# Forward transforms four quads behind the outputs instead of three, and one load issued earlier, in a spectral attention block

## The chip, the cores and the metric

The kernel runs on one core of a Trainium2 chip. The metric is the device time of one execution in microseconds (us), median of several runs; lower is better.

## The reference

The input x is (4, 64, 256, 256) in float32: four batches of 64 images of 256 x 256 pixels. Cut to what matters:

```python
def _spec_conv(x, w1, w2, out_hw, bias=None):
    xf = jnp.fft.rfft2(x, norm='forward')
    ... # keep the lowest modes, multiply by w1 and w2
    y = jnp.fft.irfft2(out_ft, s=(Ho, Wo), norm='forward')

def tno_forward(x, ...):
    xa_n = _inorm(xa, norm1_w, norm1_b)
    k, q, v = ... # three _spec_conv of every image, 8 x 8 modes
    dprod = softmax(einsum('batd,basd->bats', q, k) * 64)   # 64 x 64 images of one batch
    att = einsum('bats,basd->batd', dprod, v)
    att = _inorm(att, an_w, an_b) + xa
    att_n = _inorm(att, norm2_w, norm2_b)
    mix = _spec_conv(att_n, mix_w1, mix_w2, (H, W), bias=mix_bias)   # 32 x 32 modes
    mixed = _inorm(mix + skip, mix_norm_w, mix_norm_b)
    return _inorm(mixed, mon_w, mon_b) + att

x = x + tno_forward(_gn(x), ...)      # _gn: group norm over width groups of 8, all images of a batch
```

The attention of a batch and its group norm need all 64 images of the batch, so nothing of a batch can be put out before the last image of it has been transformed.

## The kernel before

All 64 images of a batch lie in SBUF in one buffer X (128 partitions, two rows of the image each). A pair is two images (32 pairs, 512 KB each), a quad is four (16 quads). There is only one X: an image of the next batch is loaded over an image of this batch once that one has been stored.

TensorE (PE in the profile) does for each pair a `forward` (L342, sixteen records in the trace on L350, X times the Fourier table into a bank of psY). ScalarE (ACT) squares the images (L554) and copies psY into Y (`keep_y`, L546), and VectorE (DVE) sums the squares (L872). When all pairs of a batch are through, `attend` computes the norms, the 64 x 64 attention on low modes and the first coefficients. Then `produce` (L492 on PE, L1110 on DVE, L643 on ACT) walks over the quads with a counter u:

- for u in 0 to 15, PE does `inverse_w` twice (L404) and `inverse_h` of the next quad once (L389), GpSimd (POOL) scales the four images in X (L784), and VectorE adds the synthesis from PSUM to X (`finish`, L836; semaphore `out_made`). `inverse_w(s)` waits for `out_made` of image 2s - 3, because it reuses four PSUM banks.
- from u = LAG on, PE also does the `forward` of two pairs of the next batch ahead of these inverses; those forwards go on until u = 15 + LAG. LAG is 3. In the last batch there are no such forwards.

So a produce has three phases: a head (u below LAG) with inverses alone, a middle with both, and a tail (u above 15) with forwards alone. Which comes first on each engine is written out by hand. Some work of the second group of coefficients hangs on the same counter through `second(b)`, which is LAG in all but the last batch: `energy`, `spread` and `turn_low` on PE at second, second + 3 and second + 4, `deviations`, `coefficients`, `keep_spread` and `add_low` on DVE at second to second + 4, and `low_piece(b, 2)` on ACT at second + 5, whose result `inverse_h` of quad 10 reads at u = 9. POOL waits for `coef_made` before image 4 * LAG + 12 (L799).

All image transfers are issued by SyncE (SP) on one queue: `store` waits for `out_made`, `reload` waits for the store of the same pair. After store q of a batch comes the reload of pair q - 1. The first and the last two pairs are moved in halves of one image.

There are three places where a batch hands over to the next. They are called the first, second and third handover here; the last batch has none. In the first its head begins at about 115 us and its tail ends at 232 us of the span.

Of the kernel before, what the change touches and what calls it, by code (L numbers as in the profile page):

```python
# [13 lines left out]
U0 = 8  # L14
PAIRS, QUADS, NG = IMGS // 2, IMGS // 4, IMGS // 8
TABLES = 15
LAG = 3
RING = 4
QRING = 8
HALVED = (0, PAIRS - 2, PAIRS - 1)  # L20
# [54 lines left out]
def spectral_block(nc, x, mix_re, mix_im, mix_mirror, low_w, low_mix, scalars,  # L75
# [8 lines left out]
    with ctx:  # L84
# [158 lines left out]
        def second(b):  # L243
            return LAG if b < B - 1 else 1

# [29 lines left out]
        @block.sync  # L275
        def _(sp):
            def load_images(nb, n0, n1, done):
                sp.dma_start(Xf[:, n0:n1, :], x_v[nb, :, n0:n1, :]).then_inc(done, 16)

            def store_images(b, n0, n1, done):  # L280
                sp.wait_ge(out_made, 64 * b + n1)
                sp.dma_start(out_v[b, :, n0:n1, :], Xf[:, n0:n1, :]).then_inc(done, 16)

            def load(nb, q):
                if q in HALVED:
                    load_images(nb, 2 * q, 2 * q + 1, load_first[q])
                    load_images(nb, 2 * q + 1, 2 * q + 2, load_done[q])
                else:
                    load_images(nb, 2 * q, 2 * q + 2, load_done[q])

            def reload(nb, q):
                if q in HALVED:
                    sp.wait_ge(store_first[q], 16 * nb)
                    load_images(nb, 2 * q, 2 * q + 1, load_first[q])
                    sp.wait_ge(store_done[q], 16 * nb)
                    load_images(nb, 2 * q + 1, 2 * q + 2, load_done[q])
                else:
                    sp.wait_ge(store_done[q], 16 * nb)
                    load_images(nb, 2 * q, 2 * q + 2, load_done[q])

            def store(b, q):
                if q in HALVED:
                    store_images(b, 2 * q, 2 * q + 1, store_first[q])
                    store_images(b, 2 * q + 1, 2 * q + 2, store_done[q])
                else:
                    store_images(b, 2 * q, 2 * q + 2, store_done[q])

            flat = lambda t: t.rearrange("p r n -> p (r n)")
            small = [(GWT[:, :, :, :, :].rearrange("p a b n v -> p (a b n v)"), t_w), (flat(INVH[:, :, :]), t_inv_h),
                     (INVW[:, :], t_inv_w), (GROUP[:, :], t_group), (EYE[:, :], t_eye), (SEL[:, :], t_sel),  # L310
                     (SIDE[:, :], t_side), (PAIR[:, :], t_pair), (ROWS[:, :], t_rows), (SC[:, :], scalars),
                     (MRE, mix_re), (MIM, mix_im), (MMIR, mix_mirror), (flat(LM[:, :, :]), low_mix),
                     (LW[:, :, :, :].rearrange("p n r k -> p (n r k)"), low_w)]
            sp.dma_start(FWD[:, :, :].rearrange("p a n -> p (a n)"), t_fwd).then_inc(fwd_in, 16)
            for q in range(PAIRS):
                load(0, q)
                for dst, src in small[5 * q - 40:5 * q - 35] if q >= 8 else ():
                    sp.dma_start(dst, src).then_inc(tables_in, 16)  # L318

            def batch(b, more):  # L320
                for q in range(PAIRS - 2):
                    store(b, q)
                    if more and q:
                        reload(b + 1, q - 1)
                for q in range(PAIRS - 2, PAIRS):
                    store(b, q)
                for q in range(PAIRS - 3, PAIRS) if more else ():
                    reload(b + 1, q)

            for b in range(B):  # L330
                batch(b, b < B - 1)
            for q in range(PAIRS):
                sp.wait_ge(store_done[q], 16 * B)
            for q in HALVED:
                sp.wait_ge(store_first[q], 16 * B)
# [3 lines left out]
        def _(pe):  # L339
            mm = nc.tensor.matmul  # L340

            def forward(nb, p):  # L342

                if not (isinstance(nb, int) and nb == 0 and p < 2):
                    pe.wait_ge(y_kept, 32 * nb + p - 1)
                for i in range(2):
                    pe.wait_ge(loaded(2 * p + i), 16 * nb + 16)
                    for c in range(WC):
                        for a in range(HC):
                            last = mm(psY[p % 2][:, (2 * i + c) * 128:(2 * i + c + 1) * 128],  # L350
                                      X[:, 2 * p + i, a, c * 128:(c + 1) * 128], FWD[:, a, :],
                                      start=a == 0, stop=a == HC - 1)
                last.then_inc(y_made, 1)

            def add_squares(nb, k):

                if nb:
                    pe.wait_ge(t_kept, 32 * (nb - 1) + min(2 * (k + LAG + 1) + 2, 32))
                pe.wait_ge(q_summed, 64 * nb + 4 * k + 4)
# [132 lines left out]
            def produce(b, more):  # L492
                for u in range(QUADS + (LAG if more else 0)):
                    new = more and u >= LAG
                    if new:
                        if u == LAG:
                            pe.wait_ge(mode_weighted, 8 * b + 8)
                        forward(b + 1, 2 * (u - LAG))
                        if u == LAG + 1:
                            pe.wait_ge(var_made, 2 * b + 2)  # L500
                        if u == LAG + 4:
                            pe.wait_ge(c2_kept, 2 * b + 2)
                        if u == LAG + 5:
                            pe.wait_ge(d_added, 6 * b + 6)
                        forward(b + 1, 2 * (u - LAG) + 1)
                    if new and u > LAG:
                        add_squares(b + 1, u - LAG - 1)
                    if u < QUADS:
                        inverse_w(b, 2 * u)
                        if u + 1 < QUADS:  # L510
                            inverse_h(b, u + 1)
                        if new and u in (LAG, LAG + 3, LAG + 4):
                            pe.wait_ge(y_kept, 32 * (b + 1) + 2 * (u - LAG) + 2)
                        if u == second(b):
                            energy(b, 1)
                        if u == second(b) + 3:
                            spread(b, 1)
                        if u == second(b) + 4:
                            turn_low(b, 1)
                        inverse_w(b, 2 * u + 1)  # L520
                if more:
                    add_squares(b + 1, QUADS - 1)
# [665 lines left out]
```

## Time and profile before

| | |
|---|---|
| median of 3 runs | 677.81 us (675.39 to 679.09) |
| profiled execution | 681.9 us, span 679.9 us |
| mean granted TensorE clock | 0.984 of full speed |
| PE, PEld busy | 94%, 86% of the span |
| DVE, POOL, ACT busy | 72%, 52%, 49% |
| DMA queue of the images | 135.36 MB, mean 199 GB/s over the span |

The span is the stretch that the trace covers; the time of the same execution is 2.0 us longer. A busy share is a mean over stages with different limits: the DMA engines are idle in each attend and almost always busy in each produce.

### The profile page before, as it was taken

The page shows a single profiled execution, that of the slowest core. Times are in us where ns is not written, and L with a number is a line of the kernel's source. Part 1 is how long each engine was busy: PE and PEld are TensorE (multiplying, and loading weights), DVE is VectorE, ACT ScalarE, POOL GpSimd, SP SyncE. Part 2 cuts the span into 40 slices and gives each one's busy share as a digit, 9 for nine tenths or more (in the row PEclk, how much of TensorE's full clock was granted, in tenths as well). Part 3 has the DMA queues.
Part 4 walks back from the last instruction along what each step waited for, and adds up shares of the span by engine and source line. Part 5 has one row for each costly group of instructions (what it writes and reads, how often), then busy time and mean ns, then how long its engine had stood idle before and what let it go on. Part 6 is the DMA issues. An engine that isn't in the chain of part 4 may idle for free.

```text
span 679.9 us, 15103 instructions
## 1 busy us (share of the span) xinstructions
PE 636.5 (94%) x5736; PEld 581.6 (86%) x5736; DVE 487.8 (72%) x1099; ACT 334.3 (49%) x722; POOL 356.1 (52%) x430
## 2 busy tenths in 40 slices
PE   9999999899999799979999899989999989995984
PEld 9999998699999799869999789969899988994863
DVE  4667676688777567668777666857887666778896
ACT  6888142465666413255666523246566650433331
POOL 0350035959960013796993002398799000359995
PEclk9999999899999899999999999999999989999997
DMA  9990000998999200299999900059989960004786
GB/s 320 350 379 9 1 2 20 308 314 294 310 318 328 94 1 1 77 308 343 286 328 309 322 14 1 2 198 331 321 285 325 308 218 1 1 1 162 280 302 247
DMA packets 72071, 136.32 MB, mean 200 GB/s; under 512 B 5760, under 2 KB 6272, under 8 KB 72000
## 3 DMA queue, kind: packets, MB, share of 16 engines
q1 hardware_dynamic: 72000, 135.36, 58.5%
q8 instruction: 46, 0.75, 0.4%
q14 instruction: 25, 0.20, 0.1%
HBM read 68.23 MB, written 67.11 MB: 199 GB/s over the span
## 4 chain that ended last, share of the span: by engine, by line
PE 58%; DVE 15%; POOL 9%; DMA 8%; issue 3%; ACT 3%; SPq 3%; POOLq 0%; DVEq 0%; ACTq 0%
PE psY L350 23%; PE psP L404 12%; POOL X L784 7%; PE psY L373 6%; DMA X<-in_x 6%; PE psT L389 5%; PE psP L454 5%; DVE QP L872 4%; ACT SQ L554 2%; PE psP L373 2%; DVE Y L836 2%; DVE SQ L836 2%; DMA out<-X 2%; SPq L318 2%; DVE X L836 1%
## 5 line engine op out<-in xcount | busy, mean ns | idle before, releaser
L350 PE MATMUL psY<-FWD,X 128*128 128x128 f32 x2048 | 251.1, 281 | 17.5 <-DMA X<-in_x 17.4
L350 PEld LDWEIGHTS psY<-FWD,X 128*128 128x128 f32 x2048 | 238.8, 195 | 33.0 <-issue 33.0
L784 POOL TENSOR_TENSOR X<-X,ALPHA 128x512 f32<-128x512 f32 x244 | 254.7, 1080 | 21.7 <-DVE IM L1072 19.7
L872 DVE TENSOR_REDUCE QP<-SQ 128x32 f32<-128x512 f32 x256 | 162.1, 679 | 57.8 <-ACT SQ L554 57.8
L836 DVE TENSOR_TENSOR X<-X,psP 128x512 f32<-128x512 f32 x192 | 126.5, 684 | 59.9 <-PE psP L404 26.1
L554 ACT ACTIVATE SQ<-X 128x512 f32<-128x512 f32 x256 | 146.4, 622 | 21.1 <-DMA X<-in_x 14.4
L404 PE MATMUL psP<-INVW,T 64*128 64x256 f32 x768 | 141.3, 402 | 12.0 <-DVE X L836 11.3
L762 POOL TENSOR_TENSOR Y<-Y,OMEGA 128x256 f32<-128x256 f32 x32 | 25.3, 790 | 215.9 <-ACT Y L558 215.6
L404 PEld LDWEIGHTS psP<-INVW,T 64*128 64x128 f32 x768 | 92.9, 190 | 31.2 <-issue 16.0
L576 ACT ACTIVATE T<-psT,BIA,SCL 128x256 f32<-128x256 f32 x128 | 65.3, 560 | 110.3 <-PE psT L389 105.8
L546 ACT ACTIVATE Y<-psY 128x512 f32<-128x512 f32 x128 | 76.2, 596 | 60.4 <-PE psY L350 59.6
L373 PE MATMUL psY<-GWR,Y 128*128 128x128 f32 x768 | 93.2, 279 | 0.0
L373 PEld LDWEIGHTS psY<-GWR,Y 128*128 128x128 f32 x768 | 87.8, 192 | 4.1 <-issue 3.0
L404 PE MATMUL psB<-INVW,T 64*128 64x256 f32 x256 | 69.7, 393 | 0.0
L389 PE MATMUL psT<-INVH,Y 64*128 64x256 f32 x512 | 67.1, 378 | 0.0
L389 PEld LDWEIGHTS psT<-INVH,Y 64*128 64x128 f32 x512 | 51.3, 189 | 4.8
L767 POOL TENSOR_TENSOR Y<-Y 128x256 f32<-128x256 f32 x32 | 23.8, 743 | 47.1 <-DVE Y L836 47.1
L404 PEld LDWEIGHTS psB<-INVW,T 64*128 64x128 f32 x256 | 46.1, 188 | 0.0
L836 DVE TENSOR_TENSOR X<-X,psB 128x512 f32<-128x512 f32 x64 | 43.6, 682 | 3.1 <-POOL X L784 2.6
L454 PEld LDWEIGHTS psP<-GWR,Y 128*64 128x64 f32 x272 | 30.5, 204 | 2.4 <-DVE GWR L839 2.4
L563 ACT ACTIVATE Y<-Y 128x128 f32<-128x128 f32 (+2 forms) x44 | 12.9, 294 | 39.4 <-DVE Y L836 28.5
L454 PE MATMUL psP<-GWR,Y 128*64 128x64 f32 x272 | 31.1, 275 | 0.8 <-DVE GWR L839 0.8
(189 smaller groups left out, 478.8 us busy)
## 6 DMA issues: line engine op xcount, KB each, us to landing
X<-in_x SPq DMA_DIRECT2D x116, 512.0 KB, 5.5
out<-X SPq DMA_DIRECT2D x116, 512.0 KB, 4.4
X<-in_x SPq DMA_DIRECT2D x24, 256.0 KB, 5.2
out<-X SPq DMA_DIRECT2D x24, 256.0 KB, 3.7
INVH<-t_inv_h SPq DMA_DIRECT2D x1, 256.0 KB, 9.6
LW<-in_low_w SPq DMA_DIRECT2D x1, 204.0 KB, 6.6
GWT<-t_w SPq DMA_DIRECT2D x1, 192.0 KB, 9.9
FWD<-t_fwd SPq DMA_DIRECT2D x1, 128.0 KB, 2.1
```

The costliest lines, as they stand in the source:

```text
L350: last = mm(psY[p % 2][:, (2 * i + c) * 128:(2 * i + c + 1) * 128], X[:, 2 * p + i, a, c * 128:(c + 1) * 128], FWD[:, a, :], start=a == 0, ...
L373: last = mm(over(psM[g % 3][:, col:col + 1], [[256, 2], [1, 64]]), both[:, c, k, :], over(GWR[:, c, k, 0, 0:1], [[NV, 2], [1, 2 * NV]]), s ...
L389: last = mm(psT[h][:, 0:H], S[rows, q, part, :, :].rearrange("p j n -> p (j n)"), INVH[rows, part, :], start=part == 0, stop=part == 1)
L404: last = mm(out_bank(b, 2 * s + i)[:, W * a:W * (a + 1)], T[rows, s % 4, 128 * a:128 * (a + 1)], INVW[rows, :], start=True, stop=True)
L454: last = mm(ps[0:IMGS, col:col + 64], Y[:, c, k, :, U0 + n], GWR[:, c, 0, k:k + 2, :], start=c == 0, stop=c == WC - 1)
L546: nc.scalar.activation(Y[:, :, :, i0:i0 + 3:2, :].rearrange("p c k i u -> p i (c k) u"), psY[p % 2][:, :].rearrange("p (i n u) -> p i n u" ...
L554: nc.scalar.activation(SQ[:, n % RING, :], Xf[:, n, :], ACT.Square).then_inc(squared, 1)
L576: nc.scalar.activation(T[:, p % 4, :], psT[p % 2][:, 0:H], ACT.Identity, bias=BIA[:, p:p + 1], scale=SCL[:, p:p + 1]).then_inc(t_kept, 1)
L762: P.tensor_tensor(v, v, over(OMEGA[:, 0:1], [[0, 4], [0, 2], [1, NV]]), MUL).then_inc(powers_weighted, 1)
L784: P.tensor_tensor(v, v, al, MUL).then_inc(x_scaled, 1)
L836: return V.tensor_tensor(out, a, b, op)
L872: V.tensor_reduce(QP[:, 4 * (k % 2) + place(n) % 4, :], SQ[:, n % RING, :].rearrange("p (a g j) -> p g a j", a=HC, j=GW), AX.XY, ADD).then ...
```

## The change

LAG becomes 4. The head of the first three batches is then four quads long, the middle has twelve quads instead of thirteen, and the tail has four quads of forwards instead of three. The steps that hang on second(b) and on LAG move one quad later with it: so does POOL's wait for `coef_made`, from image 24 to image 28. In the store and reload loop, reload 29 is issued between the stores of pair 30 and those of pair 31, instead of after both.

```diff
-LAG = 3
+LAG = 4
...
             def batch(b, more):
-                for q in range(PAIRS - 2):
+                for q in range(PAIRS):
                     store(b, q)
                     if more and q:
                         reload(b + 1, q - 1)
-                for q in range(PAIRS - 2, PAIRS):
-                    store(b, q)
-                for q in range(PAIRS - 3, PAIRS) if more else ():
-                    reload(b + 1, q)
+                if more:
+                    reload(b + 1, PAIRS - 1)
```

On PE, at the end of the first head, the program before runs the inverses of quad 2 and then the first forwards of batch 1 (rows on L350; L404 is `inverse_w`, L389 `inverse_h`).

```order
L404 MATMUL psP<-INVW,T 128x256 [waits out_made,t_kept]
L404 MATMUL psB<-INVW,T 128x256
L404 MATMUL psP<-INVW,T 128x256
L404 MATMUL psB<-INVW,T 128x256
L350 MATMUL psY<-FWD,X 128x128 [waits load_first0,y_kept,mode_weighted]
L350 MATMUL psY<-FWD,X 128x128 x3
L350 MATMUL psY<-FWD,X 128x128 [waits load_done0]
L350 MATMUL psY<-FWD,X 128x128 x3
L350 MATMUL psY<-FWD,X 128x128 [waits load_done1,y_kept]
```

In the changed kernel (its lines are two lower: L402, L387, L348) the same place reads as follows.

```order
L402 MATMUL psP<-INVW,T 128x256 [waits out_made,t_kept]
L402 MATMUL psP<-INVW,T 128x256 x3
L387 MATMUL psT<-INVH,Y 128x256 [waits t_kept]
L387 MATMUL psT<-INVH,Y 128x256 x3
L402 MATMUL psP<-INVW,T 128x256 [waits out_made,t_kept]
L402 MATMUL psB<-INVW,T 128x256
L402 MATMUL psP<-INVW,T 128x256
L402 MATMUL psB<-INVW,T 128x256
L348 MATMUL psY<-FWD,X 128x128 [waits load_first0,y_kept,mode_weighted]
L348 MATMUL psY<-FWD,X 128x128 x3
L348 MATMUL psY<-FWD,X 128x128 [waits load_done0]
```

The eight matrix products of quad 3's two `inverse_w` and the four of `inverse_h` now stand ahead of the first forward, which itself is unchanged and waits for the same loads.

On SP, at the end of a batch, the program before has the following.

```order
L278 DMA X<-in_x 128x2x512 [waits store_done28]
L282 DMA out<-X 128x512 [waits out_made] x4
L278 DMA X<-in_x 128x2x512 [waits store_done29]
L278 DMA X<-in_x 128x512 [waits store_first30]
L278 DMA X<-in_x 128x512 [waits store_done30]
```

The changed kernel has this in its place.

```order
L278 DMA X<-in_x 128x2x512 [waits store_done28]
L282 DMA out<-X 128x512 [waits out_made] x2
L278 DMA X<-in_x 128x2x512 [waits store_done29]
L282 DMA out<-X 128x512 [waits out_made] x2
L278 DMA X<-in_x 128x512 [waits store_first30]
```

The load of pair 29 no longer stands behind the two stores of pair 31, and those two now stand behind it.

## Rows read from the trace of the kernel before

**Rows 1.** The page's first part: busy us, share, instructions.

```profile
PE 636.5 (94%) x5736; PEld 581.6 (86%) x5736; DVE 487.8 (72%) x1099; ACT 334.3 (49%) x722; POOL 356.1 (52%) x430
```

**Rows 2.** Waits of all engines: us in total, times, longest us.

```profile
PE psY L350 <- DMA X<-in_x: 17.4, 9, 3.2
```

**Rows 3.** Waits of SP's own queue, same columns.

```profile
SPq L282 <- DVE X L836: 416.6, 117, 73.3
```

**Rows 4.** PE's timeline, first handover's head: start, us, line, idle before.

```profile
124.59 2.02 PE L350 MATMUL psY<-FWD,X 128*128 128x128 f32 x16 [0.32 <-DMA X<-in_x]
128.63 2.73 PE L350 MATMUL psY<-FWD,X 128*128 128x128 f32 x16 [2.01 <-DMA X<-in_x]
...
135.39 3.84 PE L350 MATMUL psY<-FWD,X 128*128 128x128 f32 x32
...
142.07 3.84 PE L350 MATMUL psY<-FWD,X 128*128 128x128 f32 x32
```

**Rows 5.** PE's timeline, heads of the second and third handover.

```profile
295.36 2.02 PE L350 MATMUL psY<-FWD,X 128*128 128x128 f32 x16 [2.26 <-DMA X<-in_x]
...
300.51 3.73 PE L350 MATMUL psY<-FWD,X 128*128 128x128 f32 x31
...
307.19 3.06 PE L350 MATMUL psY<-FWD,X 128*128 128x128 f32 x25
...
458.87 2.02 PE L350 MATMUL psY<-FWD,X 128*128 128x128 f32 x16 [2.70 <-DMA X<-in_x]
...
470.70 2.50 PE L350 MATMUL psY<-FWD,X 128*128 128x128 f32 x20
```

**Rows 6.** DVE's timeline: finish of image 11 in the three heads.

```profile
129.20 0.69 DVE L836 TENSOR_TENSOR X<-X,psB 128x512 f32<-128x512 f32 x1 [0.35 <-POOL X L784]
...
294.78 0.69 DVE L836 TENSOR_TENSOR X<-X,psB 128x512 f32<-128x512 f32 x1 [0.34 <-POOL X L784]
...
458.96 0.69 DVE L836 TENSOR_TENSOR X<-X,psB 128x512 f32<-128x512 f32 x1 [0.34 <-POOL X L784]
```

**Rows 7.** PE's timeline, first and second tail: first quad, longest wait, end.

```profile
216.49 3.84 PE L350 MATMUL psY<-FWD,X 128*128 128x128 f32 x32
...
224.88 3.35 PE L350 MATMUL psY<-FWD,X 128*128 128x128 f32 x16 [2.54 <-DMA X<-in_x]
...
232.16 0.28 PE L361 MATMUL psT<-ONES,QP 128*128 128x1 f32 x2
...
381.61 3.84 PE L350 MATMUL psY<-FWD,X 128*128 128x128 f32 x32
...
390.69 2.02 PE L350 MATMUL psY<-FWD,X 128*128 128x128 f32 x16 [3.23 <-DMA X<-in_x]
...
396.35 0.28 PE L361 MATMUL psT<-ONES,QP 128*128 128x1 f32 x2
```

**Rows 8.** SP's timeline, end of the first handover's transfers.

```profile
216.52 2.32 SPq L282 DMA_DIRECT2D out<-X  x4
218.88 3.52 SPq L278 DMA_DIRECT2D X<-in_x  x5
```

**Rows 9.** Windows: busy us of each engine, granted clock, DMA share, GB/s.

```profile
121.00:138.00 17.00, 14.53 (x105) 12.30 (x106) 10.88 (x20) 8.04 (x19) 16.68 (x20) 0.90 1.00 328
143.00:216.00 73.00, 73.00 (x691) 66.90 (x691) 55.46 (x100) 46.48 (x89) 47.66 (x50) 1.00 0.92 308
```

**Rows 10.** Windows after the first and the second head's wait.

```profile
128.60:132.00 3.40, 3.37 (x20) 3.09 (x22) 3.05 (x6) 1.66 (x3) 3.40 (x4) 0.67 1.02 327
...
295.40:298.80 3.40, 3.40 (x30) 3.15 (x32) 2.69 (x6) 1.60 (x3) 3.40 (x4) 1.00 0.92 308
```

**Rows 11.** POOL's timeline at its wait for `coef_made`, first handover.

```profile
151.32 8.51 POOL L784 TENSOR_TENSOR X<-X,ALPHA 128x512 f32<-128x512 f32 x8 [7.10 <-DVE IM L1072]
```

**Rows 12.** Timelines of PE and ACT at u = 8, first handover.

```profile
163.94 3.84 PE L350 MATMUL psY<-FWD,X 128*128 128x128 f32 x32
...
165.47 0.28 ACT L563 ACTIVATE Y<-Y 128x96 f32<-128x96 f32 x1 [2.66 <-DVE Y L836]
```

## The prediction

> **What bounds the kernel now.** I read the page first. PE is busy for 94% of the span, far ahead of DVE with 72% [rows 1], so whatever does not remove idle time or slow clock from PE can hardly shorten the run. Next I asked the list of waits what stops PE. Its largest entry with a releaser that this change touches is the forward waiting for a load of X: 17.4 us in nine waits [rows 2]. The order in time shows that these sit at two places of every handover: two in the head, when the first pairs of the next batch have not yet landed, and one in the tail, when pair 29 has not. In between PE has no gap at all: in the 73 us from 143 to 216 it is busy for 73.00 us [rows 9]. SP on its side waits mostly for outputs (416.6 us, most of it in the attends, [rows 3]), so in the middle the transfers follow PE and not the other way round.
>
> The head is slower than PE alone would be. The finishes of its images are released by POOL's scaling [rows 6], which takes about 1.06 us an image (8.51 us for eight, [rows 11]). PE has some 3 us of work in such a quad (worked out below), so it idles there anyway.
>
> **What the change does to the head.** PE gets quad 3's inverses ahead of the first forward. Their last wait is for the finish of image 11, which the change does not touch: it ends at 129.20 + 0.69 = 129.9, 295.5 and 459.65 us [rows 6]. The second `inverse_w` then takes 1.1 us, so the first forward starts at 131.0, 296.6 and 460.75. By then both pairs have landed: PE began on pair 1 at 128.63, 295.36 and 458.87 right after its landing [rows 4, 5]. The two pairs take 3.8 us as in the undisturbed quads [rows 4]. The inverses that follow take 300.51 - (295.36 + 2.02) = 3.1 us at full clock [rows 5]. So u = 4 ends at 137.9, 303.5 and 467.65. Before, it ended at 142.07, 307.19 and 470.70 [rows 4, 5]. That is 4.2, 3.7 and 3.05 us earlier, 10.9 us in all. It is the size of one pair of forwards moved out (3.8 us) plus waits and slow clock saved, minus the extra time at POOL's pace.
>
> **What it does to the middle.** Eleven quads are left after u = 4 in both versions, with the same work, and I take their 74.4 us (142.07 to 216.49) as they are. Three covers are needed for that.
>
> The loads: pair 2 is wanted at 137.9 instead of 135.39. For every later pair it is the same: outputs, and with them stores and reloads, come 3.0 to 4.2 us sooner, and the forward comes one quad (6.7 us) later behind them, so each load has 6.7 us more between its pair's outputs and its use, and is used 2.5 to 3.6 us later on the clock than now.
>
> The third piece of low modes: `low_piece(b, 2)` moves from u = 8 to u = 9, and `inverse_h` of quad 10 reads it in that same u = 9. Before, ACT started it 165.47 - 163.94 = 1.5 us after PE's quad began [rows 12], and it is two such instructions of 0.28 us. PE wants it after two forwards and one `inverse_w`, 4.9 us after the quad began. Since it is ready 2.0 us after the quad began, the cover shrinks from a quad and more to 2.9 us, but does not vanish. Behind that wait would stand the rest of PE's quad and all stores.
>
> POOL's pause: it stood idle for 7.10 us before image 24 [rows 11]. It now does four more images (4.2 us at the rate of [rows 11]) first and pauses before image 28, one quad later, so the distance to the finish that reads the first image after the pause is unchanged.
>
> **What it does to the tail.** PE goes through four quads of forwards at 3.82 us, 15.3 us, if no load is late. Before it took 232.16 - 216.49 = 15.7 us in the first handover and 396.35 - 381.61 = 14.7 us in the second [rows 7]; the third is like the first (15.5). So the tail itself gives +0.5 at worst and -0.4 at best, together nothing. Are the loads in time? Pair 29 was issued at 218.88, 2.4 us after the tail began, and PE started on it 8.4 us after the tail began [rows 7, 8]. Now PE wants it 9.5 us after the tail began. The reordering brings its issue forward by about 1.2 us, the time between the second and the fourth store of that burst [rows 8]. The halves of pairs 30 and 31 are still gated by their own stores; they kept up with PE from 224.88 on, and are wanted 11.5 and 13.4 us into the tail. All have 1 to 3 us to spare, so the 2.5 and 3.2 us waits go. The reordering alone I therefore cost at nothing here: the longer tail covers it. The two stores of pair 31 that it passes are delayed by one issue of 0.4 us, inside that room. Without the longer tail it would be worth up to 1.2 us a handover.
>
> **The clock.** In the first head, PE's granted clock fell to half (1.2 GHz of 2.4) for about 3.4 us after the wait: the window of 128.6 to 132.0 shows a mean of 0.67 [rows 10]. From 128.63 to the next quad's forward it took 6.76 us, against 5.15 us in the second handover with a clock of 1.00 [rows 4, 5, 10]. Such a fall costs 1.6 us. In the first tail it did so too (forward of one pair 3.35 us against 2.02, [rows 7]), in the second it did not, after a longer wait. The changed head has one idle stretch instead of two, from the end of quad 2 to the finish of image 9. In the first handover that is from 124.59 - 0.32 = 124.3 [rows 4] to 129.9 less two finishes at POOL's pace, 127.8 [rows 6], or 3.5 us. Of the two waits in heads shown at [rows 4, 5] with 2.01 and 2.26 us the shorter was followed by a fall, and of the two in tails again the shorter; so it is a matter of chance here, half and half. I book one fall for the three new heads, +1.6 us, between nothing and three (4.8 us). The saved one of the first head is inside the 4.2 us above.
>
> The Trainium skill (TensorE: Matmul & The Clock Gate, Part 1) says that the array's clock is gated down when PE has not been busy lately, and that a loop that waits for DMA can swing between the two rates; by it three falls rather than one, 3.2 us less gain. This trace bears it out only in part: the second handover had waits of 2.26 and 3.23 us and kept a clock of 1.00.
>
> **The sum.** 10.9 us from the heads, 0 from the tails, 1.6 us back for the clock: 9.3 us. Against the profiled execution's 681.9 us that gives 672.6; the median of the runs lies 4.1 us lower, so I predict 677.8 - 9.3 = 668.5 us.
>
> **Rivals.**
>
> *Transfers bind.* In the head the DMA engines are full (share 1.00) at 328 GB/s, and the middle takes 308 with a share of 0.92 [rows 9]. Outputs now come 4.2 us sooner, 1.3 MB at 308 GB/s, and the queue can catch up by 20 GB/s times 73 us, 1.5 MB. That is just enough. If the rate can't rise over 308 at all, the last loads land when they do now: pair 29 at 224.8 in the first handover, where PE wants it at 212.3 + 9.5 = 221.8. The gain there falls by 3 us, similarly in the others: 3 us in all, 674.8. For it speaks the share of 0.92; against it that SP waits for outputs, that is, requests are missing and not bandwidth. In between lie 3 to 9 us.
>
> The Trainium skill (DMA: Bandwidth & Descriptors, Specifications) gives about 358 GB/s as the limit of HBM for one core. By that the room would be 50 GB/s, 3.6 MB, and this rival would be out. The measured 328 with engines full is less.
>
> *The clock falls in every new head and more often elsewhere.* Three falls: 10.9 - 4.8 = 6.1 us, 671.7. With none: 666.9.
>
> *Slower.* The one mechanism that could do it is the third piece at u = 9. If `low_piece` is ready later than PE's `inverse_h` wants it by d in each handover, the gain shrinks by 3d. It decides at d = 9.3/3 = 3.1 us, and for a loss over 0.5% (3.4 us) at d = 12.7/3 = 4.2 us, that is when it is ready 7.1 us later in its quad than now; with d = 5 the time would be 683.5 us. ACT does its two copies (L576) before it and they wait for PE's previous quad, so I see no reason for that [rows 12].
>
> *No effect.* If the extra head quad took a full 6.7 + 1 us because PE's inverses wait for more than POOL, each head's gain is 1 us or so, 3 us in all. The finish rows of POOL's pace speak against it [rows 6].
>
> **How the numbers follow.** My forecast (7 to 12 us gained): 0.62. Transfers bind, partly or wholly (1 to 6 us): 0.17. Falls in every head (about 6 us): 0.10. No effect or little (within 3.4 us): 0.06. Slower: 0.05. The range of 662.5 to 675 us takes in no fall and some gain from neighbouring runs below, and the whole of the transfer rival above. A measurement tells 0.5% (3.4 us) from no change. Faster by more than that: 0.62 + 0.10 + about half of the transfer rival and a bit, 0.83; within: 0.12; slower: 0.05.
>
> **What would show it.** In the new profile the forward's wait for X (17.4 us) should be near zero, PE should idle before `inverse_w` in the heads on DVE and POOL instead, each tail should last 15.3 us with no gap, and the distance between the first heads' end and the tails' begin should be unchanged. Loads late in the tail would show the transfer rival, a granted clock of 0.5 after the heads the second, a wait of `inverse_h` for ACT L563 the third. The prediction is wrong if the first forward does not start about 6 us later than now, or if the middle's quads get longer than 6.7 us.

## The result: 0.5% faster, not 1.4%

The median of 20 runs of the changed kernel is 676.5 us, of 20 runs of the kernel before 679.6 us. The ratio is 0.9951, 95% interval 0.9928 to 0.9974: 3.3 us (1.8 to 4.9), where 9.3 were forecast. The median also lies above the stated range of 662.5 to 675 us. The profiled execution took 675.3 us with a span of 673.4, 6.5 us less than the one before. That pair shows more than the medians do: the profiled execution before lies 2.3 us above the median of its 20 runs, the one after 1.2 us below its own.

The page after, first part, answers to [rows 1].

```profile
PE 637.8 (95%) x5736; PEld 582.5 (86%) x5736; DVE 490.0 (73%) x1099; ACT 333.2 (49%) x722; POOL 356.1 (53%) x430
```

PE is busy 1.3 us longer with the same 5736 records, in a shorter span, so some of its work has got slower. The last batch alone has 2.0 us of that, and cost no time: the windows from the end of the third tail to the end of the span, before and after, are as long as each other, at a lower granted clock (the column before the last two).

```profile
560.58:679.90 119.32, 98.93 (x893) 84.94 (x891) 91.43 (x221) 33.90 (x95) 75.79 (x84) 0.95 0.38 142
554.14:673.40 119.26, 100.89 (x893) 86.35 (x891) 91.41 (x221) 33.89 (x95) 75.69 (x84) 0.93 0.38 142
```

The list of waits after, between 110 and 600 us (the three handovers), has no row of PE waiting for X, where before there were 16.9 us in that stretch and 17.4 in the whole span [rows 2]. So what the change was made for came true. In its place PE waits for DVE; before and after, in the same stretch:

```profile
PE psP L404 <- DVE X L836: 0.4, 2, 0.2
PE psP L402 <- DVE X L834: 11.4, 5, 3.7
```

PE's timeline of the first head after answers to [rows 4]. The number in brackets is the idle time before the group.

```profile
127.72 1.19 PE L402 MATMUL psP<-INVW,T 64*128 64x256 f32 x8 [3.67 <-DVE X L834]
128.66 1.96 PE L387 MATMUL psT<-INVH,Y 64*128 64x256 f32 x8
...
132.20 3.84 PE L348 MATMUL psY<-FWD,X 128*128 128x128 f32 x32
...
139.17 3.84 PE L348 MATMUL psY<-FWD,X 128*128 128x128 f32 x32
```

One idle stretch of 3.67 us, then an `inverse_h` that takes 1.96 us instead of 1.03. The forwards start at 132.2, where the prediction had 131.0, and u = 4 ends at 139.17 (137.9). The other two heads have the same form, and the second is worse:

```profile
290.05 2.08 PE L402 MATMUL psP<-INVW,T 64*128 64x256 f32 x8 [3.67 <-DVE X L834]
291.88 1.95 PE L387 MATMUL psT<-INVH,Y 64*128 64x256 f32 x8
295.47 4.04 PE L348 MATMUL psY<-FWD,X 128*128 128x128 f32 x32
...
302.64 3.84 PE L348 MATMUL psY<-FWD,X 128*128 128x128 f32 x32
...
453.51 2.08 PE L402 MATMUL psP<-INVW,T 64*128 64x256 f32 x8 [3.67 <-DVE X L834]
...
464.65 3.84 PE L348 MATMUL psY<-FWD,X 128*128 128x128 f32 x32
```

The windows after each head's stretch answer to [rows 10]; the column after the busy times is the mean granted clock, 1.00 for 2.4 GHz and 0.50 for 1.2.

```profile
127.70:131.10 3.40, 3.38 (x20) 3.30 (x22) 2.14 (x4) 0.44 (x1) 3.40 (x5) 0.64 1.10 371
...
290.00:293.40 3.40, 3.35 (x16) 2.97 (x18) 2.13 (x4) 0.00 (x0) 3.40 (x5) 0.50 1.01 372
293.40:296.80 3.40, 3.40 (x21) 2.57 (x19) 1.82 (x3) 2.46 (x6) 3.24 (x5) 0.63 0.97 296
...
453.50:456.90 3.40, 3.39 (x18) 3.02 (x20) 2.17 (x4) 0.00 (x0) 3.40 (x5) 0.58 1.04 366
```

The clock fell to half in all three new heads, in the second for twice as long. The tail has no gap, which answers to [rows 7] (216.49 to 232.16 before):

```profile
213.59 3.84 PE L348 MATMUL psY<-FWD,X 128*128 128x128 f32 x32
...
228.65 0.28 PE L359 MATMUL psT<-ONES,QP 128*128 128x1 f32 x2
```

That is 15.06 us, and the other two tails took the same. The middle is as it was: 139.17 to 213.59 is 74.42 us, as from 142.07 to 216.49 before.

### The profile page after: what moved, and what is told of

It reads as the page before. It is cut to its first block, busy times and chain, and to the rows that moved or that the text cites. A ratio compares the mean times of both kernels' runs of the same rounds, so it can differ in the third digit from the quotient of the medians.

```text
span 673.4 us, 15100 instructions
## 1 busy us (share of the span) xinstructions
PE 637.8 (95%) x5736; PEld 582.5 (86%) x5736; DVE 490.0 (73%) x1099; ACT 333.2 (49%) x722; POOL 356.1 (53%) x430
## 4 chain that ended last, share of the span: by engine, by line
PE 53%; DVE 20%; POOL 17%; ACT 5%; issue 4%; DMA 1%; SPq 0%; POOLq 0%; DVEq 0%; ACTq 0%
PE psY L348 20%; POOL X L782 12%; PE psP L402 11%; DVE QP L870 9%; PE psT L387 5%; PE psP L452 5%; PE psY L371 5%; ACT SQ L552 4%; DVE Y L834 3%; PE psP L371 2%; DVE SQ L834 2%; DVE X L834 1%; POOL ALPHA L775 1%; POOL Y L765 1%; POOL ALPHA L772 1%
## 5 line engine op out<-in xcount | busy, mean ns | idle before, releaser
L348 PEld LDWEIGHTS psY<-FWD,X 128*128 128x128 f32 x2048 | 234.6, 192 | 14.8 <-issue 14.6
L348 PE MATMUL psY<-FWD,X 128*128 128x128 f32 x2048 | 245.8, 279 | 0.7 <-DMA X<-in_x 0.6
L402 PE MATMUL psP<-INVW,T 64*128 64x256 f32 x768 | 144.9, 410 | 20.5 <-DVE X L834 19.7
L760 POOL TENSOR_TENSOR Y<-Y,OMEGA 128x256 f32<-128x256 f32 x32 | 23.8, 744 | 207.3 <-ACT Y L556 207.0
L402 PEld LDWEIGHTS psP<-INVW,T 64*128 64x128 f32 x768 | 95.5, 194 | 41.0 <-issue 24.8
L402 PE MATMUL psB<-INVW,T 64*128 64x256 f32 x256 | 71.5, 401 | 0.0
L387 PE MATMUL psT<-INVH,Y 64*128 64x256 f32 x512 | 70.5, 393 | 0.0
L387 PEld LDWEIGHTS psT<-INVH,Y 64*128 64x128 f32 x512 | 53.7, 197 | 5.3
L765 POOL TENSOR_TENSOR Y<-Y 128x256 f32<-128x256 f32 x32 | 25.2, 786 | 47.6 <-DVE Y L834 47.6
L402 PEld LDWEIGHTS psB<-INVW,T 64*128 64x128 f32 x256 | 47.4, 194 | 0.0
```

The source lines that it names most:

```text
L387: last = mm(psT[h][:, 0:H], S[rows, q, part, :, :].rearrange("p j n -> p (j n)"), INVH[rows, part, :], start=part == 0, stop=part == 1)
L402: last = mm(out_bank(b, 2 * s + i)[:, W * a:W * (a + 1)], T[rows, s % 4, 128 * a:128 * (a + 1)], INVW[rows, :], start=True, stop=True)
L765: P.tensor_tensor(S[:, 2 * g:2 * g + 2, 0, :, :].rearrange("p q j n -> p q (j n)"), w[:, 0, :].rearrange("p (q n) -> p q n", q=2), w[:, 1, ...
```

## The experiments

Each kernel is compared with the kernel before on the same chip; the ratio and its 95% interval are given. The median of the kernel before in the three groups (e1 to e4, e5 to e8, e9 to e12) was 680.1, 680.3 and 681.0 us.

### The two edits apart

**e1**: the lag alone, against the kernel before.

```diff
-LAG = 3
+LAG = 4
```

> Only LAG is 4; the stores and reloads stand in the old order. Theory (the longer tail covers the loads, the order edit is hidden): no forward waits for X in the tails, each tail lasts 15.1 us as in the changed kernel, and the time is that of the changed kernel, ratio to before 0.995 within 0.002. Rival (the order edit carries the measured gain): a wait for X of 1 us or more in the tails and a ratio of 1.00.

Measured: 675.9 us, ratio 0.9957 (0.9936 to 0.9978), the same as with both edits. PE has no wait for X in the handovers, and its first tail has no gap:

```profile
214.03 3.84 PE L350 MATMUL psY<-FWD,X 128*128 128x128 f32 x32
...
229.09 0.28 PE L361 MATMUL psT<-ONES,QP 128*128 128x1 f32 x2
```

15.06 us again, without the order edit. The theory held in this trace: behind the longer tail the order edit is hidden. The clock fell in all three heads here too.

**e2**: the order of stores and reloads alone. The cut shows the edit against the changed kernel.

```diff
-LAG = 4
+LAG = 3
```

> Only the order edit, with LAG 3. Theory: pair 29 is issued some 1.2 us sooner, its wait in each tail falls from 2.5 to 3.2 us to 1.3 to 2 us, heads unchanged; 3 us less at most, ratio 0.996. Rival (the queue is full at the end of a batch and the load lands when it did): the waits in the tails are as before, ratio 1.00.

Measured: 674.3 us, ratio 0.9924 (0.9891 to 0.9956). That is 5.2 us less (3.0 to 7.4), by the ratio more than both edits give together, though the intervals overlap. The theory had 3 us at most, which the interval just takes in. PE's first tail in its timeline:

```profile
215.36 3.84 PE L348 MATMUL psY<-FWD,X 128*128 128x128 f32 x32
...
219.17 4.09 PE L348 MATMUL psY<-FWD,X 128*128 128x128 f32 x32
...
223.24 2.03 PE L348 MATMUL psY<-FWD,X 128*128 128x128 f32 x16
225.61 2.02 PE L348 MATMUL psY<-FWD,X 128*128 128x128 f32 x16 [0.33 <-DMA X<-in_x]
227.47 0.77 PE L359 MATMUL psT<-ONES,QP 128*128 128x1 f32 x4
```

The wait of 2.54 us ahead of pair 29 [rows 7] is gone; what is left is scattered over this tail in pieces of 0.3 us, and no fall of the clock follows. PE starts on pair 29 some 5.9, 6.8 and 7.0 us into the three tails, against 8.4, 9.1 and 8.5 before. That is more than the 1.2 us a handover that the prediction gave it. SP's timeline shows one half of it.

```profile
215.38 0.95 SPq L282 DMA_DIRECT2D out<-X  x2
216.98 0.39 SPq L278 DMA_DIRECT2D X<-in_x  x1
217.42 0.97 SPq L282 DMA_DIRECT2D out<-X  x2
```

The load of pair 29 is issued 1.6 us after the tail began, against 2.4 in [rows 8], and in the other two handovers 1.0 and 1.4 against 2.9 and 2.3. That is 1.2 us sooner on average, as the prediction had it, and 3.5 in all. The other half is the time from issue to landing, the last number of these rows: first the kernel before in its three handovers, then e2.

```profile
X<-in_x SPq DMA_DIRECT2D x1, 512.0 KB, 5.9
X<-in_x SPq DMA_DIRECT2D x1, 512.0 KB, 6.1
X<-in_x SPq DMA_DIRECT2D x1, 512.0 KB, 6.0
X<-in_x SPq DMA_DIRECT2D x1, 512.0 KB, 4.1
X<-in_x SPq DMA_DIRECT2D x1, 512.0 KB, 5.6
X<-in_x SPq DMA_DIRECT2D x1, 512.0 KB, 5.5
```

Together 2.8 us less, most of it in the first handover. The program now puts two half stores directly ahead of this load instead of four, which would explain it: over the four traces with the old order (before, e1, e4, e12) the same load took 5.9 us on average, over the ten with the new one 5.1. No run separates this from the earlier moment of issue. The prediction counted the earlier issue alone.

### The clock

**e3**: the changed kernel with idle matrix products between quad 2 and quad 3 of the first three batches. They write to psY[0], which nobody reads before the next forward overwrites it.

```diff
+            def fill(b, n, bank, free):
+                pe.wait_ge(mode_weighted, 8 * b + free)
+                for _ in range(n):
+                    mm(bank[:, 0:256], ONES[:, :], FWD[:, :, :].rearrange("p a n -> p (a n)"), start=True, stop=True)
...
+                    if more and u == 3:
+                        fill(b, 6, psY[0], 7)
                     if u < QUADS:
                         inverse_w(b, 2 * u)
```

> The changed kernel with six idle matrix products (3.0 us, the results are never read) on PE between quad 2 and quad 3 of each of the first three heads, where PE idles 3.67 us. Theory (falls of the clock in the three new heads, 1.3, 2.7 and 1.2 us, ate half of the forecast gain): the clock stays at 1.00 in those heads, first forwards start at 131.0 instead of 132.2 in the first handover, and the time is 5 us under the changed kernel's, ratio to before 0.987 to 0.989. Rival (the gain is lost elsewhere, and the falls fill time that POOL's pace would take anyway): clock stays up and the ratio stays at 0.995.

Measured: 672.1 us, ratio 0.9894 (0.9853 to 0.9934). The first head and the window behind its idle stretch:

```profile
124.13 2.86 PE L437 MATMUL psY<-FWD,ONES 128*128 128x256 f32 x12
127.88 1.13 PE L402 MATMUL psP<-INVW,T 64*128 64x256 f32 x8 [0.89 <-DVE X L841]
128.81 1.06 PE L387 MATMUL psT<-INVH,Y 64*128 64x256 f32 x8
131.00 3.84 PE L348 MATMUL psY<-FWD,X 128*128 128x128 f32 x32
...
137.97 3.84 PE L348 MATMUL psY<-FWD,X 128*128 128x128 f32 x32
```

```profile
127.70:131.10 3.40, 3.16 (x25) 2.48 (x25) 2.09 (x4) 1.19 (x4) 3.40 (x5) 1.00 1.10 384
```

With PE kept busy the clock stays at 1.00 in all three heads. The forwards start at 131.0 and u = 4 ends at 137.97, as the prediction worked out for full clock (131.0 and 137.9). The other two heads have the same form:

```profile
288.86 1.14 PE L402 MATMUL psP<-INVW,T 64*128 64x256 f32 x8 [0.90 <-DVE X L841]
298.95 3.84 PE L348 MATMUL psY<-FWD,X 128*128 128x128 f32 x32
450.05 1.14 PE L402 MATMUL psP<-INVW,T 64*128 64x256 f32 x8 [0.89 <-DVE X L841]
460.14 3.84 PE L348 MATMUL psY<-FWD,X 128*128 128x128 f32 x32
```

From the end of the stretch to the end of u = 4 all three heads take 10.09 us here. In the changed kernel they take 11.45, 12.59 and 11.14, which is 1.4, 2.5 and 1.0 us more, 4.9 in all. So the times worked out for the heads were right, and the falls are what the sum lacked. By the ratios e3 is 3.9 us below the changed kernel, with intervals that overlap a little. Waits for X of 2.0 us in all are back in its third tail.

**e4**: the kernel before with the same function at its two waits for X.

```diff
                     pe.wait_ge(y_kept, 32 * nb + p - 1)
+                if nb and p in (1, 29):
+                    fill(nb - 1, 4 if p == 1 else 5, psY[1], 8)
```

> The kernel before with idle matrix products in the two places of each handover where PE waits for X: four (2.0 us) before the forward of pair 1 and five (2.5 us) before that of pair 29, results never read. Theory: it removes the falls of the clock in heads and tails, of which the profile had three at 1.3 to 1.6 us, and adds at most 0.5 us where a wait was shorter than the filling: 3 to 4 us less, ratio 0.994 to 0.996. Rival (the kernel before keeps its clock in most runs): ratio 1.00 or above.

Measured: 675.4 us, ratio 0.9936 (0.9916 to 0.9957). That is 4.3 us less (2.9 to 5.7), about what the theory gave, and the trace shows no fall of the clock in the handovers, where the kernel before had three: in the first head and in the first and third tail.

**e8**: the changed kernel once more.

> The changed kernel itself on the same chip as the other three. By its 20 runs: ratio 0.995, mean clock 0.978 to 0.982, falls of the clock in all three new heads. If falls were chance, as the prediction took them, some head would keep its clock in this second trace.

Measured: 676.4 us, ratio 0.9950 (0.9931 to 0.9968). Its three heads in windows:

```profile
128.30:131.70 3.40, 3.36 (x21) 3.25 (x23) 2.13 (x4) 0.56 (x2) 3.40 (x5) 0.66 1.00 369
290.60:297.40 6.80, 6.77 (x33) 5.61 (x34) 3.97 (x7) 2.45 (x6) 6.64 (x9) 0.55 1.03 331
454.20:457.60 3.40, 3.40 (x18) 3.05 (x20) 2.17 (x4) 0.00 (x0) 3.40 (x5) 0.57 1.02 351
```

The same three falls, the second again the longer one. With e1 that makes nine heads of nine. The three traces repeat each other so closely that they are hardly nine separate draws, but half and half does not describe them. How many heads fall in the runs without a trace is not known: their mean granted clock goes from 0.974 to 0.986 in the changed kernel's 20 runs.

### POOL's part of the new idle stretch

**e5**: the changed kernel with POOL's last two small steps moved from ahead of image 8 to ahead of image 12.

```diff
-                behind = {2: SPLIT + 1, 8 if b < B - 1 else 3: SPLIT + 2}
+                behind = {2: SPLIT + 1, 12 if b < B - 1 else 3: SPLIT + 2}
...
-                    if u == (2 if more else 1):
+                    if u == (3 if more else 1):
                         fold_powers(b, SPLIT + 2)
```

> The changed kernel with POOL's last pair of small steps (weigh and add_products, 1.4 us) moved from ahead of image 8 to ahead of image 12, and DVE's fold of it from u = 2 to u = 3. Theory (in the new heads PE's idle stretch is set by POOL's scaling and these steps): the stretch falls from 3.67 to about 2.3 us, the first forward comes 1.4 us sooner in each head, and the clock falls less often or not at all; 4 to 7 us under the changed kernel, ratio to before 0.985 to 0.989. Rival (it is only moved to the next quad, where the same 1.4 us are paid by PE): ratio 0.995.

Measured: 670.8 us, ratio 0.9882 (0.9847 to 0.9917). The first head:

```profile
126.48 1.62 PE L402 MATMUL psP<-INVW,T 64*128 64x256 f32 x8 [2.31 <-DVE X L834]
127.83 1.98 PE L387 MATMUL psT<-INVH,Y 64*128 64x256 f32 x8
130.96 3.84 PE L348 MATMUL psY<-FWD,X 128*128 128x128 f32 x32
```

The stretch is 2.31 us as forecast and the forwards start 1.24 us earlier than in the changed kernel. But the clock fell in all three heads nevertheless, so the gain over the changed kernel, 4.6 us by the ratios, is about the three times 1.4 us of the shorter stretches; the theory was wrong on the clock. This kernel has no wait for X in the handovers. In the second head the fall lasted 3.4 us here, not 6.8.

**e6**: e5 with four idle products.

```diff
+                    if more and u == 3:
+                        fill(b, 4, psY[0], 7)
```

> As e5, with four idle matrix products (2.0 us, results never read) in the stretch that is left. Theory: no fall of the clock in the three heads, first forwards at about 129.6 us in the first handover; ratio 0.984 to 0.987. If e5 alone already keeps its clock, both are the same.

Measured: 668.7 us, ratio 0.9839 (0.9809 to 0.9869), with the clock at full in the three heads. It is the lowest ratio of the set, though its interval overlaps those of e5 and e7. **e10** repeats it:

> The best so far again: 0.984 to 0.986. With the heads 1.4 us shorter each, waits for X of about 1 us are left in some tails, since the transfers now follow closely.

Measured: 671.0 us, ratio 0.9849 (0.9798 to 0.9899). In its second tail waits for X are back:

```profile
384.75 2.02 PE L348 MATMUL psY<-FWD,X 128*128 128x128 f32 x16 [0.94 <-DMA X<-in_x]
...
389.11 2.02 PE L348 MATMUL psY<-FWD,X 128*128 128x128 f32 x16 [0.33 <-DMA X<-in_x]
```

In all it waits 4.7 us for X in the three handovers, and e6 waits 3.5. This suggests that the faster heads have used up the room in the transfers, but e5, whose heads are nearly as fast, has no such wait.

### Is the longer lag worth anything when the clock holds?

**e7**: the order edit with LAG 3, three idle products ahead of pair 1.

```diff
+                if nb and p == 1:
+                    fill(nb - 1, 3, psY[1], 8)
```

> The order edit with LAG 3 and three idle matrix products (1.5 us, results never read) ahead of the forward of pair 1 in each head, where PE waits 1.8 us for X. Theory (without falls of the clock the longer lag is still worth 2 to 3 us more than the order edit): ratio 0.990 to 0.992, above the 0.9894 of the filled kernel with LAG 4. Rival (the order edit is all that is needed): 0.989 or less.

Measured: 670.7 us, ratio 0.9867 (0.9839 to 0.9895). The rival on record was right: with the clock held, the order edit at LAG 3 is no worse than LAG 4 (e3, 0.9894). The intervals overlap, so three more kernels were run side by side.

**e9** is e3 again, **e11** is e7 again, and **e12** is e3 with the old order of stores and reloads.

> The filled kernel with LAG 4 and the new order again, beside the one with LAG 3. If the longer lag is worth something once the clock holds, this one is lower than the filled order edit by 2 us or more; the earlier runs had 0.9894 and 0.9867 the other way round, with overlapping intervals.

> The filled order edit with LAG 3 again: 0.987 if the longer lag is worth nothing with the clock held, 0.990 or more if it is.

> LAG 4 and the filling, with the stores and reloads in the old order. Theory (with the longer tail the order edit is hidden also when the heads are faster): as the same kernel with the new order, ratio 0.989, no wait for X of 1 us or more in the tails. Rival (faster heads bring the last loads close to PE): waits in the tails and 1 to 3 us more.

| | lag | order | fill | median us | ratio (95%) |
|---|---|---|---|---|---|
| e9 | 4 | new | yes | 671.6 | 0.9861 (0.9815 to 0.9907) |
| e11 | 3 | new | yes | 672.0 | 0.9861 (0.9816 to 0.9905) |
| e12 | 4 | old | yes | 672.0 | 0.9870 (0.9809 to 0.9931) |
| e4, from the first group | 3 | old | yes, at both waits | 675.4 | 0.9936 (0.9916 to 0.9957) |

Between the first three these runs can tell no difference. e12 had no wait of PE for X in the handovers, so its theory held as well. e9 waited 3.3 us for X, e11 7.4. The last row is the corner that is missing otherwise: the clock is held and neither edit is made. Its ratio, to the kernel before on its own chip, lies above those of e7, e9 and e11 beyond the intervals, and above those of e3 and e12 with intervals that overlap a little. So with the clock held the edits are still worth some 3 to 5 us.

In none of the fifteen new heads with idle products (e3, e6, e9, e10, e12) did the clock fall.

## Why the prediction was wrong

**What bounds.** Right. The waits for X in the handovers were 16.9 us before and none after.

**The heads.** The term was 10.9 us at full clock, 4.2 + 3.7 + 3.05. e3 confirms it: its first head ends within 0.1 us of the time worked out, and the other two take as long. What was wrong is the next term.

**The clock: the step that failed.** "I book one fall for the three new heads, +1.6 us." u = 4 ended at 139.17 in the first head (137.9 worked out), 1.3 us late. In the second it ended at 302.64; the worked-out 303.5, less the 3.5 us by which the first handover had ended sooner, is 300.0, so 2.6 us late. In the third it ended at 464.65 against 467.65 - 4.2 = 463.4, or 1.2 us late. Together 5.1 us instead of 1.6; the comparison with e3 gives 4.9.

The stretch the change would make was worked out in the prediction as 3.5 us in one piece (3.67 measured). It was then judged by waits of 2.0 to 3.2 us in the kernel before, which stood between forwards, and called chance. Among those waits the record is indeed mixed: after 2.01, 2.54 and 2.60 us the clock fell, after 2.26, 2.70 and 3.23 us it did not. The new stretch stands between inverses, and there it fell nine times of nine, and in e5 three times of three with 2.31 us, while with idle products in the stretch it never did. So the idle stretch is what brings the fall. That inverses around it make the difference to the waits of similar length is a guess that no run tested. The Trainium skill (TensorE: Matmul & The Clock Gate, Part 1) says that the array's clock is gated down when PE has not been busy lately. The changed kernel agrees with it in all nine heads; the six waits in the kernel before don't tell by their length which would fall. The rival "The clock falls in every new head and more often elsewhere" stood at 0.10 with a gain of 6.1 us. Its first half is what happened, and the spans of the two profiled executions differ by 6.5 us.

**The tails.** "Together nothing" for three tails at 15.3 us: they took 15.06 each, 0.7 us better in all. Right.

**The sum against the profiled execution** comes to 10.9 - 5.1 + 0.7 = 6.5 us, which is what the spans differ by. The last batch took the same time in both.

**From there to the medians** 3.3 us are left of 6.5. Here the prediction's second weak step is: it took the whole gain over to a median although the profiled execution was 4.1 us above the median shown, which was a sign that it held more waiting and falls than usual. The median itself, of three runs, was 1.8 us lower than that of 20 runs, so of the 8.0 us by which 668.5 was missed 1.8 are in the starting point.

The clock does not explain the 3.2 us that are missing between the spans and the medians. The median of the mean granted clock is 0.981 in the changed kernel's 20 runs and 0.985 in the 25 runs of the kernel before beside e1 to e4. With the rest of the time at half speed, that is 2 x 0.019 x 676 = 25.7 us against 2 x 0.015 x 680 = 20.4 us, 5.3 us more, which costs at most 2.6 us. In the two profiled executions it is 0.978 and 0.984, by the same sum 29.6 against 21.8 us, 7.8 us more. So the profiled pair carried more slow clock than the medians and still gained more. And part of it costs nothing, as the last batch shows. In e2 the median is 0.989. Where the 3.2 us went stays open; that they are luck of one execution was not tested.

**The reordering.** "I therefore cost at nothing here: the longer tail covers it" was right (e1 against both). "Without the longer tail it would be worth up to 1.2 us a handover" was too small by the trace: PE gets to pair 29 1.5 to 2.5 us sooner, 1.2 us of it by the earlier issue and the rest by the shorter time to landing; and with the waits the falls go. By the ratio it is 5.2 us, and the interval (3.0 to 7.4) still holds the three times 1.2.

**The rivals.** Transfers bind: not in the changed kernel, whose middle moved 323 GB/s where 308 had been [rows 9], so the queue did catch up. It came true in part where the clock was held: 2.0 us of waits for X in e3, 3.3 in e9, 3.5 in e6 and 4.7 in e10, though none in e12. The third piece at u = 9: ACT started it at 169.24, 1.5 us into PE's quad (167.71), exactly as in [rows 12], and no one waited. POOL's pause before image 28 cost nothing either.

So the change has two edits that cure the same wait in the tail. The order edit does it for free and leaves most of the waits in the heads. The longer lag removes both, but concentrates PE's idle time in one stretch, and pays for it in clock. Together they show no more than the order edit alone (0.9950 against 0.9924, intervals overlapping), and once the clock is held the three ways cannot be told apart.

## What to carry to other kernels

When a change moves idle time instead of removing it, ask what the new stretch looks like in one piece, and cost a clock fall for each such stretch (here 1.2 to 2.6 us) unless a row of the same form shows otherwise. A late load at the end of a batch should first be cured in the queue's order, by looking at what stands ahead of it both in the issuing program and in the queue, before the pipeline is made deeper. A few matrix products without a reader, placed into a known wait and shorter than it, can be worth as much as the restructuring: here 3 to 6 us of 680 (e3 against the changed kernel, e4 against the kernel before, e6 against e5, e7 against e2, e9 against e8).

## What was unexpected

The clock fell in the second head for twice as long as in the first, in all three traces with the 3.67 us stretch (windows 290.0 to 296.8 above; 290.6 to 297.4 in e8, mean 0.55), and once in the third (e1). In the kernel before, a 3.23 us wait in the second tail between forwards left the clock at 1.00 [rows 7], while one of 2.54 us in the first tail did not, nor one of 2.60 us in the third:

```profile
553.57 3.38 PE L350 MATMUL psY<-FWD,X 128*128 128x128 f32 x16 [2.60 <-DMA X<-in_x]
```

What decides between them is left open.
